# Four row and column sweeps on four images: the second image pair stored with alternating pixel parity, and its one-sided convolution taps sharing the array with the first pair's

## The reference, cut to what matters

```
def step(prev, row):
    new = row + relu(conv1d(prev, w, b))     # 64 x 64 channels, 9 taps along the row, padding 4
    return (new, new)
_, rest = scan(step, rows[0], rows[1:])
```

## Time and profile before

| | |
|---|---|
| median of 3 runs | 2612.29 us |
| the profiled execution | 2612.23 us, its span 2610.4 us |
| TensorE busy | 2509.8 us, 96% |
| VectorE, ScalarE, GpSimd busy | 1813.5, 1236.6, 352.7 us |
| matmul records of conv (line 870) | 40640, busy 2200.4 us |
| mean granted TensorE clock | 0.989 |

### The profile page before, as it was taken

How to read it: one execution, slowest core, us unless ns; L and a number is a source line. 1 busy time by engine, 2 the same in 40 slices (tenths; PEclk the granted TensorE clock), 3 DMA queues, 4 the chain that set the end, 5 groups by cost and what they waited for, 6 DMA issues and landing times. The chain is left out here.

```text
span 2610.4 us, 117000 instructions
## 1 busy us (share of the span) xinstructions
PE 2509.8 (96%) x46070; PEld 2417.0 (93%) x46070; DVE 1813.5 (69%) x5782; ACT 1236.6 (47%) x2705; POOL 352.7 (14%) x547
## 2 busy tenths in 40 slices
PE   1999999999999999999899999999999999998998
PEld 1389999999999999999899999999999999997885
DVE  7866666666666666677666666666666666777986
ACT  0866664222233333377666642222333333675877
POOL 1620000000000000066000000000000000653545
PEclk9999999999999999999999999999999999998999
DMA  7810001222450000087600012223600000430006
GB/s 270 219 45 0 0 0 36 61 60 60 91 54 0 0 4 1 0 258 161 190 8 0 0 29 60 60 60 88 66 0 0 0 0 0 129 97 2 4 4 258
DMA packets 323834, 155.07 MB, mean 59 GB/s; under 512 B 155169, under 2 KB 319650, under 8 KB 319650
## 3 DMA queue, kind: packets, MB, share of 16 engines
q1 hardware_dynamic: 321600, 153.41, 22.9%
q10 hardware_dynamic: 2146, 0.53, 0.1%
HBM read 70.00 MB, written 50.33 MB: 46 GB/s over the span
## 5 line engine op out<-in xcount | busy, mean ns | idle before, releaser
L870 PE MATMUL banks<-x_row,w_taps 128*64 128x124 f32 (+2 forms) x40640 | 2200.4, 270 | 5.4 <-DVE x_row L1114 3.1
L870 PEld LDWEIGHTS banks<-x_row,w_taps 128*64 128x64 f32 x40640 | 2198.8, 135 | 7.1 <-issue 6.1
L1123 DVE SCALAR_TENSOR_TENSOR x_row<-banks,sweep_nbias,biased_row 128x128 f32<-128x128 f32 x2032 | 712.9, 351 | 717.1 <-PE banks L870 695.1
L666 ACT ACTIVATE biased_row<-state,sweep_bias 128x256 f32 (+1 forms) x762 | 512.2, 673 | 1038.9 <-DVE state L1126 605.7
L662 ACT ACTIVATE biased_row<-state,aff,gn_a 128x64 f32 (+1 forms) x1016 | 364.2, 429 | 184.4 <-DVE state L1132 184.4
L1126 DVE SCALAR_TENSOR_TENSOR state<-banks,sweep_nbias,biased_row 128x128 f32 (+1 forms) x1016 | 443.0, 436 | 0.0
L550 POOL TENSOR_TENSOR state<-state,stripe_a 128x256 f32<-128x256 f32 x96 | 66.9, 733 | 1982.3 <-DVE state L1126 1962.0
L1132 DVE SCALAR_TENSOR_TENSOR state<-banks,sweep_nbias,biased_row 128x64 f32 (+1 forms) x1016 | 236.9, 275 | 0.1
L1132 DVE SCALAR_TENSOR_TENSOR turn_ring<-banks,sweep_nbias,biased_row 128x64 f32<-128x64 f32 x1016 | 236.7, 274 | 0.0
L843 PE MATMUL banks<-res,ffn_w 64*64 64x512 f32 x512 | 112.3, 597 | 6.1 <-ACT res L599 5.2
L832 PE MATMUL banks<-state,ffn_s 64*64 64x512 f32 x512 | 106.8, 598 | 0.2 <-DVE ffn_s L1285 0.2
(11 more groups left out here) (138 smaller groups left out, 903.3 us busy)
## 6 DMA issues: line engine op xcount, KB each, us to landing
state<-turn_ring SPq DMA_DIRECT2D x512, 64.0 KB, 1.9
resid<-state SPq DMA_DIRECT2D x94, 256.0 KB, 3.6
state<-x_in SPq DMA_DIRECT2D x16, 1024.0 KB, 20.7
stripe_a<-resid SPq DMA_DIRECT2D x32, 512.0 KB, 5.3
stripe_b<-resid SPq DMA_DIRECT2D x32, 512.0 KB, 5.4
out_y<-state SPq DMA_DIRECT2D x16, 1024.0 KB, 4.1
res<-resid SPq DMA_DIRECT2D x32, 256.0 KB, 7.3
resid<-state SPq DMA_DIRECT2D x16, 512.0 KB, 6.7
```

The costliest lines, as they stand in the source:

```text
L666: nc.scalar.activation(as_cells(n, biased_row[:, k, :, :]), cells(n, slice(0, B), i, k, g), ACT.Identity, bias=sweep_bias[:, n:n + 1]).the ...
L870: last = nc.tensor.matmul(out_ps[blk, :, lo:hi], w_taps[:, n % 2, s, blk], x_row[c][src][:, :, s + lo:s + hi], start=at == 0, stop=at == T ...
L1123: nc.vector.scalar_tensor_tensor(x_row[c][par][:, :, 2:2 + HALF], ps, nb, br, ALU.max, ALU.add).then_inc(row_ready[c], 1)
```

## The change

**Layout of the second pair.** In images 2 and 3 the halves of the partitions are exchanged in every other row: in odd rows the lower half holds the odd pixels. The weights of pair 1 are stored twice, once for rows of either kind: `w_taps` becomes nine taps with one empty slot beside them, shifted by one slot between the partition halves, in two versions (four DMAs for a sweep, as before).

**conv.** The two one-sided combined taps (s = 0 and s = 4) are taken apart. For output parity r, one of them is still a matmul of 128 input rows, the other is only its one quarter that is not zero, 64 x 64. A conv has so 8 matmuls 128 x 64 and 2 matmuls 64 x 64, 10 as before. Pair 0 runs its two quarters last, pair 1 runs them first; in pair 0 they lie on the diagonal of the array, in pair 1, by the exchanged parity, beside it. So the four stand together in the order and take all four quarters. TensorE now waits for `row_ready[1]` ahead of the last 128-row matmul of pair 0.

**Stores.** In the row sweeps (n % 4 < 2) VectorE no longer stores pair 1; GpSimd copies `x_row[1]` into `state`: one copy of 128 x 128 a step in the first row sweep (`store_rows`), two copies on 64 partitions in the second (`store_turned`), where they do the turn of pair 1 themselves. VectorE waits for `row_stored[1]` of two steps ago before it writes `x_row[1]`. The turn's DMAs carry half as much and wait for pair 0 alone.

**Residual.** After the FFN one DMA for each chunk keeps the rows in a new DRAM tensor `resid_rows`; `swap_back` loads the odd rows of images 2 and 3 into the exchanged halves (4 DMAs a chunk). ACT waits for chunk 0 of this before the first sweep, and in the sweep for each further chunk. `turn_residual` makes `resid` out of `resid_rows` by 64 DMAs from DRAM to DRAM while the first sweep runs. `cross` has four DMAs for two. Before the last FFN the odd pixel rows go to `resid_rows` once more and come back exchanged, by 64 DMAs that stand ahead of the output's. `gram_sb` and `o1_a` now lie in `w_taps`.

The core of the diff:

```diff
+    TURN_PARTS = 4
+    SWAP_LAG = 2
-        turn_ring = sb("turn_ring", [P, 2, 2, 2, B, WH])
-        w_taps = sb("w_taps", [P, 2, TAPS2, P])
+        turn_ring = sb("turn_ring", [P, 2, 2, 2, 2, WH])
+        w_taps = sb("w_taps", [P, 2, 2, 2 * TAPS2, C])
...
+            def swap_back(j, odd, done):
+                view = resid_rows.rearrange("p (hp r g b w) -> p hp r g b w", r=2, g=2, b=B, w=WH)
+                hp = slice(j * CR // 2, (j + 1) * CR // 2)
+                for q in range(2):
+                    into, frm = slice(q * C, (q + 1) * C), slice((1 - q) * C, (2 - q) * C)
+                    for g in range(2):
+                        sp.dma_start(state_b[into, hp, odd, g, 2:4, :].rearrange("c hp b w -> c hp (b w)"),
+                                     view[frm, hp, odd, g, 2:4, :].rearrange("c hp b w -> c hp (b w)")).then_inc(done, 16)
...
                         sp.wait_ge(row_stored[0], m * 4 + (STEPS * n + 2 * k + 1))
-                        sp.wait_ge(row_stored[1], m * 4 + (STEPS * n + 2 * k + 1))
                         turn(m, k)
...
+            sp.wait_ge(last_rows_kept, 32)
+            sp.wait_ge(kv_done, KV_TILES)
+            for j in range(CHUNKS):
+                swap_back(j, 1, rows_swapped[j])
...
+            def store_rows(layer):
+                n = 4 * layer
+                for t in range(1, H):
+                    pool.wait_ge(row_ready[1], hbase(n) + t + 1)
+                    nc.gpsimd.tensor_copy(state[:, t, :, 2:4, :], by_halves(x_row[1][t % 2][:, :, 2:2 + HALF])).then_inc(row_stored[1], 1)
...
-                        act.wait_ge(resid_stored, 16 * 4 * CHUNKS)
+                        act.wait_ge(rows_swapped[0], 64)
...
             def conv(n, c, k, hcount):
...
-                pe.wait_ge(row_ready[c], hcount)
-                for at, s in enumerate(TAP_ORDER):
-                    lo, hi = max(0, EDGE - s), min(HALF, HALF + EDGE - s)
-                    for q in range(2):
-                        blk = slice(q * C, (q + 1) * C)
-                        last = nc.tensor.matmul(out_ps[blk, :, lo:hi], w_taps[:, n % 2, s, blk], x_row[c][src][:, :, s + lo:s + hi],
-                                                start=at == 0, stop=at == TAPS2 - 1)
+                halves_of = [slice(q * C, (q + 1) * C) for q in range(2)]
+                weights = w_taps[:, n % 2, 1 if c and not par else 0]
+                crossed = c and par
+                def product(inner, r, s, start, stop):
+                    lo, hi = (0, HALF) if start else (max(0, EDGE - s), min(HALF, HALF + EDGE - s))
+                    return nc.tensor.matmul(out_ps[halves_of[1 - r if crossed else r], :, lo:hi], weights[inner, 2 * s + 1 - r, :],
+                                            x_row[c][src][inner, :, s + lo:s + hi], start=start, stop=stop)
+                def whole_taps(starting):
+                    for at in range(TAPS2 - 1):
+                        for r in range(2):
+                            if c == 0 and r and at == TAPS2 - 2:
+                                pe.wait_ge(row_ready[1], hcount)
+                            last = product(slice(0, P), r, TAP_ORDER[at] if at < TAPS2 - 2 else (0, TAPS2 - 1)[r],
+                                           starting and at == 0, not starting and at == TAPS2 - 2)
+                    return last
+                def single_taps(starting):
+                    for r, s in enumerate((TAPS2 - 1, 0)):
+                        last = product(halves_of[1 - r if c and not par else r], r, s, starting, not starting)
+                    return last
+                if c == 0:
+                    pe.wait_ge(row_ready[0], hcount)
+                    whole_taps(True)
+                    last = single_taps(False)
+                else:
+                    single_taps(True)
+                    last = whole_taps(False)
                 last.then_inc(conv_done[c], 1)
...
+                    if n % 4 < 2 and c and not (isinstance(i, int) and i * 2 + n0 + k <= 2):
+                        dve.wait_ge(row_stored[1], i * 2 + (n0 + k - 2))
                     nc.vector.scalar_tensor_tensor(x_row[c][par][:, :, 2:2 + HALF], ps, nb, br,
                                                    ALU.max, ALU.add).then_inc(row_ready[c], 1)
+                    if n % 4 < 2 and c:
+                        return
```

More of the change, by code:

```diff
@@ new lines, in _, with turn_residual, block @@
+            load_taps(1)
+            def turn_residual(hp):
+                def block(images, q, r, to_q, to_s):
+                    old = resid_rows.rearrange("(q c) (hp r g b w) -> q r hp c g b w", q=2, r=2, g=2, b=B, w=WH)
+                    new = resid.rearrange("hp (q c) s (g b w) -> q s hp c g b w", q=2, g=2, b=B)
+                    for g in range(2):
+                        sp.dma_start(new[to_q, to_s, hp, :, g, images, :].rearrange("hp c b w -> hp c (b w)"),
+                                     old[q, r, hp, :, g, images, :].rearrange("hp c b w -> hp c (b w)")).then_inc(resid_turned, 16)
@@ L342, in _ @@
-            with sp.Fori(0, CHUNKS) as j:
-                sp.wait_ge(ffn_added, j * B + B)
-                store_residual_a(j)
-            load_taps(1)
+                        block(slice(0, 2), q, r, r, q)
+                        block(slice(2, 4), q, r, q ^ r, q)
+            for part in range(TURN_PARTS):
+                turn_residual(slice(part * PAIRS // TURN_PARTS, (part + 1) * PAIRS // TURN_PARTS))
             for layer in (0, 1):
@@ L550, in add_residual, with store_turned, store @@
                         nc.gpsimd.tensor_tensor(quad_cells(z, b), quad_cells(z, b), quad_residual(z, b), ALU.add).then_inc(resid_added, 1)
+            def store_rows(layer):
[3 more added lines that the diff above has]
+                    nc.gpsimd.tensor_copy(state[:, t, :, 2:4, :], by_halves(x_row[1][t % 2][:, :, 2:2 + HALF])).then_inc(row_stored[1], 1)
+            def store_turned(layer):
+                n = 4 * layer + 1
+                low, high = slice(0, C), slice(C, P)
+                pool.wait_ge(row_stored[1], STEPS * n)
+                pool.wait_ge(biased_row_ready, row_count(n) + 1)
+                pool_done(nc.gpsimd.tensor_copy(state[high, H - 2, :, 2:4, :], state[high, H - 1, :, 2:4, :]))
+                def store(i, k):
+                    pool.wait_ge(row_ready[1], i * 2 + (hbase(n) + k))
+                    row = x_row[1][slot(n, k)]
+                    for blk, at in ((low, row_of(True, i, k)), (high, row_of(True, i, 1 - k))):
+                        if k == 0 and blk == high:
+                            pool.wait_ge(biased_row_ready, i * 2 + (row_count(n) + 1))
+                        last = nc.gpsimd.tensor_copy(state[blk, at, :, 2:4, :],
+                                                     by_halves(row[blk, :, 2:2 + HALF]))
+                    last.then_inc(row_stored[1], 1)
+                store(0, 1)
+                for i in range(1, PAIRS):
+                    for k in range(2):
+                        store(i, k)
             scale_first_row(0)
+            store_rows(0)
+            store_turned(0)
+            pool.wait_ge(row_stored[1], STEPS * 2)
             helmert_basis()
@@ L713, in rows @@
                 else:
-                    for start, stop in ((2 if n == 0 else 1, WH), (WH, PAIRS)):
+                    for start, stop in ((1, WH), (WH, PAIRS)):
                         with act.Fori(start, stop) as i:
@@ L828, in up @@
                 def up(j, b):
+                    if layer and b == 2:
+                        pe.wait_ge(rows_swapped[j], 128)
                     for q in range(2):
@@ L1169, in sweep @@
                 else:
-                    for start, stop in ((1, WH), (WH, PAIRS)):
+                    if n == 0:
+                        for k in range(2):
+                            for c in range(2):
+                                step(1, k, c, 0)
+                    for start, stop in ((2 if n == 0 else 1, WH), (WH, PAIRS)):
                         with dve.Fori(start, stop) as i:
```

97 lines of the change are left out of this document (62 added, 35 removed).

## The result

The changed kernel takes 2782.8 us (median of 4 runs, 2781.3 to 2783.1) against 2612.6: a ratio of 1.065, 95% interval 1.0635 to 1.0671. It is slower, as forecast, but by 170 us where 101 were forecast; it lies 8 us outside the range. The profiled execution has a span of 2779.4 us, 169 more than that of the kernel before.

A forecast was written before the change was run, and what follows sets the result against it. TensorE was taken to bound the kernel. Per step -0.42 + 0.22 + 0.29 + 0.01 = +0.10 us, times 1016 = +102, and -1 at the ends of stages: 2612.3 to 2713 us, range 2590 to 2775.

The forecast's parts named there:

- What bounds the kernel: In the sweeps TensorE sets the 2.16 us step, paid 1016 times; VectorE waits, so dropping its stores is worth nothing.
- GpSimd's two copies: Row copies on half the partitions in the second row sweep: 0.8 to 1.5 us, under the 2.16 us step.
- conv, removed and added: In each step's conv, four slots removed, -0.42 us; two groups of four quarters at 0.111 added, +0.22 us.
- rival 3: In conv the quarters do not share the array, 2936 us, or GpSimd or residual DMAs bind, over 2775; 4%.
- The changes of shape: Around conv's quarters, two changes a step, each 0.09 us drain plus 0.05 exposed weight load: +0.29 us, bounds 0.18 and 0.38.
- Rival 1: Shape changes around conv's quarters cost nothing: -0.19 us a step, 2418 us; 17%.
- rival 2: At conv's shape changes the array drains but weight loads are pulled ahead: -0.01 us a step, 2601 us; 9%.
- The wait that moved up: TensorE's wait for x_row[1], now ahead of pair 0's seventh slot, costs 0.01 us a step; bounds 0 and 0.04.
- Queue of the output: At the end, 64 swap DMAs delay the output's stores, but the queue catches up: +2 us, bounds 0 and 18.
- the turns: At each turn SP's four DMAs serve pair 0 alone, which is stored one conv earlier: -1 us twice.
- The start of the first sweep: ACT waits for chunk 0 alone instead of the last residual DMA ahead of the first sweep: -1.7 us.
- What would show it: Trace signs: 287 us sweeps, two PEld gaps a step, VectorE idle some 0.4 us before x_row[0]; others for wait or end mis-sized.

The follow-up runs named there:

- e10: Changed kernel with each 64-row quarter issued twice in a row, still two changes of shape a step: 3010.0 us.
- e4: Changed kernel with pair 1's quarters at the end of its conv instead of the start, giving four changes of shape a step: 3222.8 us.
- e9: Changed kernel with VectorE's wait for row_stored[1] moved from x_row[1] to behind x_row[0], ahead of pair 0's stores; all copies kept: 2738.9 us.
- e13: e9 with pair 0's two waits also exchanged, biased_row_ready named first and conv_done[0] second: 2741.2 us.
- e3: Changed kernel with the one-sided taps as 128-row matmuls with zeros in the empty half, so no quarters: 2677.3 us.
- e8: e3 with the wait for row_ready[1] back at the start of pair 1's conv: 2623.5 us.
- e15: e8 with e9's moved wait and 32 swap DMAs of two chunks for 64 of one: 2614.8 us, ratio 1.0012 to the kernel before.

## Why the prediction was right or wrong

- **What bounds the kernel**: right for the column sweeps, and VectorE's lighter load was worth nothing: it lost 198 us of work and its idle time grew. In the row sweeps of the changed kernel the loop of pair 1 through VectorE sets part of the step, the 0.087 us below. GpSimd's two copies took 0.62 us a step, not 0.8 to 1.5, which changes nothing.
- **conv, removed and added**: right. A group of four quarters is 0.112 us (e10, forecast 0.111), and four quarters do share the array: rival 3 is out.
- **The changes of shape**: right. The drain shows as 0.198 us between starts, the load as 0.05, both at both ends of the block; a change is 0.145 (e4, forecast 0.145). Rival 1 (nothing) and rival 2 (loads pulled ahead) fall with the two pauses of PEld in each step. The Trainium skill's rule in "TensorEngine Tiling (Array Packing)", Key Properties, that a change of mode drains, holds for a change of the rows alone: 0.198 us between starts where 0.105 is usual. The rule of the Trainium skill that loads are pulled ahead ("TensorE: Matmul & The Clock Gate", Part 2) does not reach over such a change: both loads of the third sweep's step stand behind a pause of 0.17 us, and the pauses of all steps add up to 346 us.
- **The stagger and the wider first taps**: missed. The sum took the four quarters as one start; they take 0.02 us to start, which is paid once a step. Together with an estimated 0.007 for 128 columns in place of 124 this covers what the column sweeps have above the forecast: +0.121 a step for +0.10. Of the sweeps' +164 us this is some 16, when 102, the 44 below and `cross`'s 2 are taken off.
- **"The wait that moved up"**: this step failed. It took VectorE's answer as 0.31 us from the rows of a kernel in which `x_row[1]` had one wait, and put the moved wait at 0.01, bounds 0 and 0.04. The bounds looked at TensorE's side only. The change also wrote a second wait ahead of `x_row[1]`, and the prediction asked only whether GpSimd would be done in time (it was), not what then carries the late wait. That came to stand on the register instruction, and `x_row[1]` came 0.403 us behind conv's last record: 0.403 + 0.35 + 0.06 is 0.81 where the wait's place is at 0.76, and the weight load shows behind it (in the second sweep the matmul that waited takes 0.319 us, the ones beside it 0.268). The row sweeps pay 0.087 a step, 508 times, 44 us (e9).
- **Queue of the output**: right in kind, mis-sized. "+2 us, bounds 0 and 18" was +6.4. The issues took 0.68 and not 0.6 us, and the queue did not catch up, since the DMA engines, not SP, had the backlog. `cross` cost 2 us and not 1, the turns gave 0.7 and 0.5 and not 1 each. The start of the first sweep did not move (-0.1 for the forecast -1.7): ACT no longer waited for a DMA there, but the FFN's last matmul ended 1.7 us later than before (135.8 for 134.2), and the coefficients with it. Why the FFN ran later was not looked into.
- **What would show it**: of the signs named, the pauses of PEld came as written, a sweep was 290 and 301 us and not 287, VectorE was idle ahead of `x_row[0]` for 0.53 us in column sweeps and 0.89 in row sweeps and not some 0.4, the output's DMAs ended more than 8 us behind the last matmul (13.2, before 5.9). One sign was useless: that `row_ready[1]` would end TensorE's waits. TensorE's matmuls overlap, and conv's group shows 3.8 us of idle time in the whole run, though 44 us went into that wait. It was to be seen only in VectorE's idle time and in the period.

Had the second wait been priced at its 44 us, the same sum would have given 2757. The range was also narrower than the bounds of its own terms: with 0.38 for the two changes and 0.04 for the wait a step is +0.22, not +0.16, and the total 2835.

## What to carry to other kernels

A saving inside a chain of matmuls is worth its columns less the changes of tiled shape it brings; here a change of shape costs 0.145 us, more than one slot, and 0.20 us of saving a step did not pay for two. Where a wait is added to an instruction on a tight chain, ask not only whether it is satisfied but which wait the instruction itself then carries. The late one belongs on it; the satisfied one costs nothing on an instruction ahead (pair 0 in every kernel but e13). A kernel that would do all of conv on quarters, and so never change the shape within a step, is left open; it wasn't tried.

## What the runs showed of the hardware that was not expected

On VectorE, the `x_row` instruction carried one wait in every kernel here, and a second one went to an instruction ahead of it. With the wait that ends last (`conv_done`) on `x_row` itself, `x_row` starts 0.313 to 0.317 us behind the last record of conv, with or without a satisfied wait ahead of it. With the late wait on a semaphore instruction ahead it is 0.382 to 0.385, with the late wait on a register instruction ahead 0.401 to 0.405. Why a register instruction costs more than a semaphore instruction (0.084 for 0.065 us) no run shows. All these are kernels with quarters. In the kernel before it is 0.307 to 0.314; in e3, e8 and e15 the latency of `x_row[1]` lies between 0.31 and 0.57 by sweep, which was not looked into.
